# New SBUF homes for the matmul operands of a fused attention and mixture-of-experts kernel

## What is computed

```
x = x + conv_attention(layernorm_over_channels(x))     # linear attention, 8 heads of 32
t = tokens(x)                                          # 16 x 1024 tokens of 128
n = layernorm(t)
w = softmax(mean_over_images(n) @ Wr + br)             # 1024 x 8, one weight per pixel and expert
h = relu(bn1(n @ W1[e] + b1))                          # for each of 8 experts, 128 x 128
h = relu(bn2(h @ W2[e] + b2))
y = h @ Wo[e] + bo
t = t + sum over e of w[:, e] * y[e]
```

## Time and profile before

| | |
|---|---|
| median of three runs | 819.18 us |
| the profiled execution's own time | 819.31 us |
| its span, first to last instruction | 817.5 us |
| TensorE busy | 789.0 us, 97% of the span, 4186 matmuls |
| VectorE, ScalarE, GpSimd busy | 541.8, 423.0, 580.3 us |
| mean granted TensorE clock | 0.995 of full speed |

### The profile page before, as it was taken

How to read it: one execution, slowest core, us unless ns; L and a number is a source line. 1 busy time by engine, 2 the same in 40 slices (tenths; PEclk the granted TensorE clock), 3 DMA queues, 4 the chain that set the end, 5 groups by cost and what they waited for, 6 DMA issues and landing times.

```text
span 817.5 us, 12753 instructions
## 1 busy us (share of the span) xinstructions
PE 789.0 (97%) x4186; PEld 667.5 (82%) x4186; DVE 541.8 (66%) x1053; ACT 423.0 (52%) x509; POOL 580.3 (71%) x494
## 2 busy tenths in 40 slices
PE   4999999999998889999999999999999999999997
PEld 3889999999997668888888888888888888888885
DVE  4668888787886746565665656656656566565663
ACT  3356565665655554554554545545455455454542
POOL 5447878878885368667766776677777776677665
PEclk9899999999999999999999999999999999999999
DMA  7124334443342250220201202102022020120100
GB/s 240 53 78 156 129 137 146 147 153 115 126 156 103 80 232 0 78 73 5 78 26 51 77 0 77 55 22 77 0 77 77 0 77 26 51 77 0 51 26 26
DMA packets 22107, 64.52 MB, mean 79 GB/s; under 512 B 2608, under 2 KB 6840, under 8 KB 22080
## 3 DMA queue, kind: packets, MB, share of 16 engines
q1 hardware_dynamic: 22080, 64.19, 21.6%
HBM read 38.98 MB, written 25.20 MB: 79 GB/s over the span
## 4 chain that ended last, share of the span: by engine, by line
PE 62%; DVE 2%; DMA 1%; POOL 1%; issue 1%; ACT 0%; SPq 0%; POOLq 0%; DVEq 0%
PE psum L530 61%; DMA x_res<-x_scratch 1%; POOL xn_lo L1024 1%; DVE st L858 0%; SPq L325 0%; POOLq L83 0%; POOL x_res L1055 0%; PE psum L485 0%; PE psum L586 0%; DVE xn2T L785 0%; DMA route_scratch<-routeT 0%; POOL ln L1003 0%; POOL xn2T L1011 0%; DVE x_res L964 0%; DVE w_raw L907 0%
## 5 line engine op out<-in xcount | busy, mean ns | idle before, releaser
L891 DVE SCALAR_TENSOR_TENSOR h_lo<-psum,h_hi 128x1024 fp32r<-128x1024 f32 x128 | 156.7, 1224 | 198.8 <-ACT h_hi L700 198.7
L700 ACT ACTIVATE h_hi<-psum 128x1024 fp32r<-128x1024 f32 x128 | 131.4, 1026 | 256.3 <-PE psum L530 256.3
L1024 POOL TENSOR_TENSOR h_lo<-w_raw,h_hi 128x1024 fp32r<-128x1024 f32 x64 | 154.2, 2410 | 48.7 <-ACT h_hi L712 48.7
L530 PE MATMUL psum<-h_hi,w_hi 128*128 128x512 f32 x384 | 119.4, 392 | 1.8 <-DVE w_raw L907 1.8
L907 DVE SCALAR_TENSOR_TENSOR w_raw<-psum,minus_t,route_all 128x1024 f32<-128x1024 f32 x94 | 119.9, 1275 | 1.7 <-DMA route_all<-route_scratch 1.7
L530 PE MATMUL psum<-h_hi,w_lo 128*128 128x512 f32 x384 | 119.6, 393 | 0.0
L530 PE MATMUL psum<-h_lo,w_hi 128*128 128x512 f32 x384 | 118.7, 390 | 0.0
L1024 POOL TENSOR_TENSOR xn_lo<-w_raw,xn_hi 128x1024 fp32r<-128x1024 f32 x32 | 78.0, 2438 | 51.6 <-ACT xn_hi L712 51.6
L1024 POOL TENSOR_TENSOR xn_lo<-feat_most,xn_hi 128x1024 fp32r<-128x1024 f32 x32 | 77.3, 2415 | 51.0 <-ACT xn_hi L712 51.0
L1003 POOL TENSOR_TENSOR ln<-ln,const 128x8 f32<-128x8 f32 x32 | 53.4, 1667 | 60.2 <-DVE ln L875 60.2
L530 PEld LDWEIGHTS psum<-h_hi,w_hi 128*128 128x128 f32 x384 | 71.8, 188 | 17.4 <-issue 2.6
(11 more groups left out here) (146 smaller groups left out, 1431.5 us busy)
## 6 DMA issues: line engine op xcount, KB each, us to landing
route_all<-in_x SPq DMA_DIRECT2D x16, 512.0 KB, 3.9
x_res<-in_x SPq DMA_DIRECT2D x16, 512.0 KB, 3.3
x_scratch<-x_res SPq DMA_DIRECT2D x16, 512.0 KB, 2.8
xn_scratch<-xn SPq DMA_DIRECT2D x16, 512.0 KB, 2.6
xs_in<-xn_scratch SPq DMA_DIRECT2D x16, 512.0 KB, 4.5
x_res<-x_scratch SPq DMA_DIRECT2D x16, 512.0 KB, 3.3
out<-x_res SPq DMA_DIRECT2D x15, 512.0 KB, 2.6
route_all<-route_scratch SPq DMA_DIRECT2D x6, 512.0 KB, 6.7
```

Source lines behind the costliest of these rows:

```text
L530: mm = pe.matmul(dst[:, px], w[:, which, e, :], part[:, px], start=first and w is w_hi and part is hi, stop=last and part is lo, skip_grou ...
L700: nc.scalar.activation(h1_hi[r][:], z1[r], ACT.Relu).then_inc(h1_hi_done, 1)
L891: nc.vector.scalar_tensor_tensor(out=h1_lo[r][:], in0=z1[r], scalar=0.0, in1=h1_hi[r][:].bitcast(F32), op0=ALU.max, op1=ALU.subtract).then ...
L1024: nc.gpsimd.tensor_tensor(h2_lo[r][:], h2w[r], h2_hi[r][:].bitcast(F32), ALU.subtract).then_inc(h2_lo_done, 1)
```

## The change

Unused tiles, called spacers, are put between the operand tiles, and some operand tiles are allocated in another order. A pair of a high and a low tile now lies together, and each pair starts at an offset of its own modulo 512 bytes. `w_lo` is moved 64 bytes on. No instruction, wait or loop changes.

```diff
+        def spacer(name, size):
+            sb(f"spacer_{name}", [128, size // 4])
+
...
         w_hi = sb("w_hi", [128, 3, EXPERTS, 128], F32R)
+        spacer("w_lo", 64)
         w_lo = sb("w_lo", [128, 3, EXPERTS, 128], F32R)
...
-        xn_hi = [sb(f"xn_hi{p}", [C, PIXELS], F32R) for p in range(2)]
-        xn_lo = [sb(f"xn_lo{p}", [C, PIXELS], F32R) for p in range(2)]
+        xn_hi, xn_lo = [None, None], [None, None]
+        for p, size in ((0, 0), (1, 128)):
+            if size:
+                spacer(f"xn{p}", size)
+            xn_hi[p] = sb(f"xn_hi{p}", [C, PIXELS], F32R)
+            xn_lo[p] = sb(f"xn_lo{p}", [C, PIXELS], F32R)
...
-        xs_hi = [sb(f"xs_hi{p}", [C, PIXELS], F32R) for p in range(2)]
-        xs_lo = [sb(f"xs_lo{p}", [C, PIXELS], F32R) for p in range(2)]
-        h1_hi = [sb(f"h1_hi{p}", [HIDDEN, PIXELS], F32R) for p in range(2)]
-        h1_lo = [sb(f"h1_lo{p}", [HIDDEN, PIXELS], F32R) for p in range(2)]
+        xs_hi, xs_lo, h1_hi, h1_lo, h2_hi, h2_lo = ([None, None] for _ in range(6))
+        for hi, lo, name, p, size in ((xs_hi, xs_lo, "xs", 0, 384), (h2_hi, h2_lo, "h2", 0, 32), (xs_hi, xs_lo, "xs", 1, 32),
+                                      (h1_hi, h1_lo, "h1", 0, 64), (h2_hi, h2_lo, "h2", 1, 64), (h1_hi, h1_lo, "h1", 1, 64)):
+            spacer(f"{name}{p}", size)
+            hi[p] = sb(f"{name}_hi{p}", [128, PIXELS], F32R)
+            lo[p] = sb(f"{name}_lo{p}", [128, PIXELS], F32R)
...
-        h2_hi = [sb(f"h2_hi{p}", [HIDDEN, PIXELS], F32R) for p in range(2)] + xn_hi
-        h2_lo = [sb(f"h2_lo{p}", [HIDDEN, PIXELS], F32R) for p in range(2)] + xn_lo
+        h2_hi += xn_hi
+        h2_lo += xn_lo
```

## The result

The changed kernel takes 824.69 us, the median of seven runs (822.62 to 827.16), beside 819.01 us for the kernel before (818.11 to 820.82). The ratio is 1.0073, with a 95% interval from 1.0054 to 1.0092: slower, by 5.7 us. I had forecast 810.

The account below looks back on a forecast made before the run. The prediction took TensorE's expert matmuls, their number times the start-to-start distance, as the bound. From 819.31 us it subtracted 8.6 for the expert matmuls and 1.0 for attention, giving 809.7, stated as 810; range 795 to 826.

Parts of the forecast that it names:

- What bounds the kernel: Expert loop: 2172 back-to-back TensorE matmuls, 229.96 ns from start to start, make 499.46 us, three fifths of the time.
- overlap of 162 ns: Expert loop: a matmul's record runs about 162 ns past the next start, so duration less 162 gives the start-to-start time.
- The pitch follows the home of the moving operand: Expert matmuls: start-to-start time depends on the moving tile's offset modulo 512 bytes, 228.8 ns at 320, 233.0 at 128.
- The value of 226 ns for unseen homes: Expert matmuls: at new, untraced tile offsets start-to-start time falls from 229.96 to 226 ns, gaining 8.6 us over 2172 matmuls.
- The two seen homes: Expert blocks at offsets already traced: xn1 moved to 320 gains 1.0 us, h1_1 moved to 128 loses 2.0 us.
- The slower rival: Expert loop: each change of tile offset between blocks costs 8 ns and most offsets are like 128; 826 us, chance 0.27.
- The excess gone altogether: Rival for the expert matmuls: start-to-start time drops to 214 ns, 34.7 us gained, 785 us; chance 0.12.
- the 214: Time in ns for a 512-column matmul at full clock, taken as half of 428 ns measured at half clock.
- What is late next: Expert loop: VectorE's weighting ends 0.48 or 0.36 us before the next layer-2 block; this cover holds with faster matmuls.
- The rule against the change: Skill page on TensorE reads: by it no tile offset could matter, so the time would stay 819.3 us.
- Attention: Attention stage: 288 matmuls reading xn save 2.3 us of TensorE time, half counted, 1.0 us gained, bounds -1.5 to 2.3.

Follow-up runs that it names:

- table of homes: Short kernel without the model: chains of 24 equal matmuls, 16 moving-operand start offsets against 4 weight offsets, other engines idle; settled at 226.7 to 234.4 ns a matmul.
- mixed chains: Short kernel without the model: weights alternating by matmul 232.2 ns, in pairs 232.5 ns, moving offset changing after every six 230.6 ns.
- kernel with h1 on 64: Kernel before, with all operand pairs at offset 320 modulo 512 bytes except h1 at 64: 817.11 us, ratio 0.998.
- homes spread by 256: Kernel before, with w_lo, h1 and xn at offset 256 and xs, h2 and w_hi at 0 modulo 512 bytes: 811.81 us, ratio 0.9900.
- 64 fine offsets: Short kernel without the model: 64 chains of 18 matmuls, weights at 0, moving operand 0 to 252 bytes behind in steps of 4; settled at 226.7 to 240.0 ns.

## Why the prediction was wrong, point by point

*What bounds the kernel* was right: the number of expert matmuls times their pitch. The full kernels moved about as their pitch did, and 2304 x 2.44 ns, 5.6 us, is about the changed kernel's loss. One reading was off: the nine forms of the earlier trace rows last 392.2 ns in the mean and not 391.5, which moves the overlap of 162 ns by under 1 and changes nothing behind it.

*The pitch follows the home of the moving operand* was half right. It follows that home less the weights' home, modulo 256 bytes. The trace of before could not tell the two apart: xn met weights on three homes, 0 in the loop, 448 (wkT) and 288 (mT) in attention, but the differences were 128, 192 and 96 modulo 256, all of a pitch of 233 ns or more. I took the agreement of 233 to 235 ns for independence from the weights, and bounded the shift of w_lo, which two of six matmuls of a block load (one pair in three, not every second one), only together with the unseen homes.

*The value of 226 ns for unseen homes* is the step that failed. That the beat of 232, 226 and 230 ns is TensorE's own and not its neighbours' was right: the table of homes has it with the other engines idle. But I read it as a lock that repeated starts cause, and the new homes as what breaks it, and put its fast member, 226 ns, on all blocks. The table shows that the beat is what a constant difference of 64 gives, 228.9 ns in the mean, and that its 226 does not come without the 229 and the 232. A pitch of 226.7 throughout comes with a difference of 0, and with no other multiple of 32 below 256; the new homes spread the differences instead, mostly onto ones of 233 to 234 ns. The table gives, with w_lo used by two of six matmuls, these pitches for the new homes: xs0 231.8, xs1 233.3, h1_0 228.9, h1_1 231.8, h2_0 234.2, h2_1 228.2, xn0 233.3, xn1 228.2. Weighted by blocks that is 231.3 ns, against 229.6 for the homes of before, so 1.7 x 2304 = 3.9 us slower. The loop's 232.1 ns leaves 0.8 ns or 1.8 us for the mixing and changing of differences, less than the mixed chains and the kernel with w_lo alone show for mixing; this second part is a remainder, not measured by itself in the changed kernel. With w_lo back, where no block mixes differences but most follow one with another, the remainder is 231.9 - 231.6 = 0.3 ns. Block by block it is not the table plus one price: in the changed kernel h1_0 took 1392 ns where the table gives 1373, xn0 1400 where it gives 1400. Why the difference of two addresses sets the pitch, no run here shows.

*The two seen homes*: xn1 on 320 was forecast at the good pitch and its blocks took 1372 ns; h1_1 on 128 was forecast to lose, and lost. The table, from the differences, gives 1369 for the one and 1391 for the other, which took 1396.

*The slower rival* came nearest. It gave 826, with 8 ns for each change of home and half of the unseen homes bad; the measured sum has two parts like these, 3.9 and 1.8 us. That the number came so near is in part luck. Address changes are free at an equal difference, as the kernel with h1 on 64 shows, and no home is bad by itself: in the table 128 takes 233.3 ns against weights on 0 and 228.9 against weights on 64. The stated range held the measured time only because it reached up to this rival.

*The excess gone altogether* does not happen at any offset tried: 226.7 ns is still 13 above the 214 that I had worked out for the columns.

*What is late next* held, but in other kernels than the changed one, whose loop got longer. At 226.7 ns, with the homes spread by 256, TensorE waits once for VectorE's weighting (0.9 us, at the end, as before), and the loop has no other wait.

*The rule against the change.* The Trainium skill, page "SBUF — State Buffer", section "Who interferes with whom", says that TensorE's ports for moving data and for weights are independent and that TensorE never waits on anyone. On the first the runs do not agree: with all other engines idle the pitch of a settled chain varied from 226.7 to 240.0 ns with the two addresses alone. On the second no run here speaks: the pitch varied with no other engine at work.

*Attention* was counted at 1.0 us gained. No run shows a gain or a loss there: from 20 to 290 us TensorE was busy for 260.11 us before and after, with 1883 and 1878 matmuls.

## What to carry to other kernels

Where a loop is bound by matmuls like these (reduced float32, 128 x 128 weights loaded for each, 512 columns, full clock), look at the start addresses of both operands. Moving start less weight start, modulo 256 bytes, was best at 0, and best kept the same for every operand in the chain. Spacers make that for 704 or 1216 bytes in a partition here, and it gave 0.8 to 1.0% of the time. Whether other types, other shapes or weights that stay loaded behave so, no run here shows. And a pattern seen on two homes says nothing of a third; a kernel of 405 us gave the whole table at once.

## What the runs showed that I had not expected

- In steps of 32 bytes the period is 256, and the best values lie at differences 0 and 64, with 32 between them slow: 226.7, 233.4 and 228.9 ns. In steps of 4 the order is finer still: 60 settles at 226.7 and 100 at 240.0.
- Of the 64 fine offsets 42 settle within 0.15 ns of 226.7, 230.0, 233.3, 236.7 or 240.0 ns, even steps of 3.3. The others lie between, as 228.9 from 232, 226 and 229. Why, no run shows.
- Two good differences in one chain can be worse than either: w_lo alone moved, to differences that are each better in the table, made the kernel slower (1.0034).
- The memory of a chain is longer than one matmul. After a change of difference up to some eight matmuls are unsettled. In the table a chain that should run at 227 began with 230, 236, 228, 233, 231, 226.
